# A one-core transformer kernel: constants loaded between the heads of the first batch, another split of the first projections, and a last output stage in which TensorE spreads the reciprocals

## The chip, the cores and the metric

The kernel runs on one core of one Trainium2 chip. The metric is device time in microseconds (us); the kernel before takes 2841.02 us, the median of three runs (2840.93 to 2844.28). Times in traces are counted from the start of the profiled span.

## The reference

The input x is [4, 1024, 128] in float32 (4 batches, 1024 tokens, 128 channels). Four attention blocks follow each other, each followed by a feed-forward block, each with its own layer norm and residual:

```python
x = x + attention_masked(layernorm(x))   # softmax, row i sees columns j >= i
x = x + ffn0(layernorm(x))               # x @ W[idx] + b[idx], idx = argmax(log_softmax(logits) + gumbel(u))
x = x + attention_rbf(layernorm(x))      # exp(-sigma * |k - q|^2) @ v, no softmax
x = x + ffn0(layernorm(x))
x = x + attention_rel(layernorm(x))      # Transformer-XL scores with a relative shift, softmax
x = x + ffn1(layernorm(x))               # x @ weight.T + (x[:64] + x[64:]) @ disha
x = x + attention_rope(layernorm(x))     # rotary q and k, softmax
x = x + ffn1(layernorm(x))
```

Every attention has 16 heads of 8 channels, projections q, k, v from 128 channels and an output projection back to 128.

## The kernel before

**Stages and rounds.** There are 4 stages (masked, RBF, relative, rotary) of 64 heads each (4 batches x 16), 256 heads in all. The work is laid out in rounds: round n computes the scores of head n with keys on the partitions (TensorE into `ring`, exponentials by ScalarE into `probs`), their product with the values (into `ppv`), and, two heads ahead, the scores of head n+2 with queries on the partitions, of which VectorE takes row maxima (`mx`, `mall`). Rounds -2 and -1 only take maxima. The maxima are split in three bf16 parts by GpSimd (`mparts`), turned by TensorE, copied by VectorE (`mrow`) and stored by a DMA into the query rows: that DMA is `place` (L639), and the next head's first score matmul waits for it. Sixteen rounds are an interval: while the heads of batch i-1 run, the layer norm, projections and operand splits of batch i are slipped in, and, two or more intervals later, the output projection and feed-forward of a finished batch.

**Who does what.** Layer norm: VectorE's statistics (L1284, L1287), four small GpSimd operations (L1571 to L1576), then `xn` by VectorE in the first batch and in two of the stages (L1296), otherwise by ScalarE. TensorE turns xn (L998), ScalarE copies it out (`xnT`, L1136), TensorE projects (L1013, L1020). float32 k and q are split in three bf16 parts each (cast, subtract, cast, subtract). In the first batch GpSimd splits k (L1646 to L1652) and VectorE splits q (L1356, L1358). Twelve DMAs of 256 KB store these parts to DRAM (`records_k`, `records_q`, L675), and the heads load them from there (L623, L624).

**SyncE's queue.** All DMAs are issued by SyncE, in program order: an issue behind a waiting one waits too. Constants fall in three semaphores: `s_c0` (those of the first projections and the masks), `s_ck` (for the choice of a feed-forward matrix), and `s_c1` (everything else). `s_c1` constants are issued partly before the first stores and partly right behind the first loads (L580), then 16 rows of ones (L596, L597). TensorE waits for all of `s_c1` ahead of round 0.

**The table of due times.** `Plan` gives each small step a tick (a slot of a round); every engine's program calls `start.go(tick)` and `finish.go(tick)` in each slot, which issue the steps that are due. `choose()` (L1414 to L1424) is VectorE's sum of the eight candidate matrices by a one-hot row, 19 small instructions spread over two rounds; before, it begins in round 2.

**The end.** After the last head its row of `heads_out` is stored, the denominators (`dens`) and the outputs (`oT`) of the last batch are loaded back, VectorE takes reciprocals (L1385), a DMA stores them (`inverses`), four DMAs load them spread over 8 partitions each (`den`), GpSimd multiplies (L1682), and then come output projection (L1058), residual (L1390), statistics, normalising, turning, feed-forward (L1067), residual (L1405) and the store of the result. All these matmuls go through the one PSUM bank `pm`, so that the second half of each step waits until the first has been taken out.

## Time and profile before

| what | value |
|---|---|
| median of 3 runs | 2841.02 us |
| the profiled execution, its own time | 2840.0 us |
| its span | 2838.2 us |
| PE busy | 2662.1 us (94%) |
| ACT busy | 2100.8 us (74%) |
| DVE busy | 2066.8 us (73%) |
| POOL busy | 905.8 us (32%) |
| mean granted clock of TensorE | 0.981 of full speed |

PE is TensorE, PEld its weight loads, DVE is VectorE, ACT is ScalarE, POOL is GpSimd, SPq is SyncE's DMA queue. A row of a timeline has start, duration, engine, line, operation, output and input, and in brackets the idle time of the engine before it and what ended it. The profiled execution took 1.8 us more than its span and 1.0 us less than the median of the three runs. Nearly the whole span is filled by TensorE; the stretches in which it is not are the first 71 us and the last 41 us.

### The profile page before, as it was taken

The page shows a single profiled execution, that of the slowest core. Times are in us where ns is not written, and L with a number is a line of the kernel's source. Part 1 is how long each engine was busy: PE and PEld are TensorE (multiplying, and loading weights), DVE is VectorE, ACT ScalarE, POOL GpSimd, SP SyncE. Part 2 cuts the span into 40 slices and gives each one's busy share as a digit, 9 for nine tenths or more (in the row PEclk, how much of TensorE's full clock was granted, in tenths as well). Part 3 has the DMA queues.
Part 4 walks back from the last instruction along what each step waited for, and adds up shares of the span by engine and source line. Part 5 has one row for each costly group of instructions (what it writes and reads, how often), then busy time and mean ns, then how long its engine had stood idle before and what let it go on. Part 6 is the DMA issues. An engine that isn't in the chain of part 4 may idle for free.

```text
span 2838.2 us, 107110 instructions
## 1 busy us (share of the span) xinstructions
PE 2662.1 (94%) x43744; PEld 1599.3 (56%) x43744; DVE 2066.8 (73%) x5515; ACT 2100.8 (74%) x3766; POOL 905.8 (32%) x1609
## 2 busy tenths in 40 slices
PE   3999998999999999999999999999999999999995
PEld 1666565655555555666666666666644444444443
DVE  4888888822222228888788888878889989999992
ACT  1777776799999996666666666666678878888883
POOL 2212132322213242722541361252136134351231
PEclk7999999999999999999999999999999999999997
DMA  6333232334424351411331241222123223232121
GB/s 175 88 95 116 85 109 79 112 104 127 128 88 121 96 160 55 125 57 55 97 89 50 72 131 50 72 81 70 45 64 106 63 63 98 64 112 63 57 71 40
DMA packets 197778, 250.62 MB, mean 88 GB/s; under 512 B 48340, under 2 KB 113748, under 8 KB 197288
## 3 DMA queue, kind: packets, MB, share of 16 engines
q1 hardware_dynamic: 197288, 243.77, 29.2%
q8 instruction: 346, 5.67, 0.9%
q14 instruction: 144, 1.18, 0.1%
HBM read 133.28 MB, written 100.14 MB: 82 GB/s over the span
## 4 chain that ended last, share of the span: by engine, by line
PE 69%; DVE 20%; issue 5%; ACT 2%; SPq 2%; DMA 1%; POOL 1%; DVEq 0%; ACTq 0%; POOLq 0%
PE ppv L977 29%; DVE mx L1244 14%; PE ring L834 6%; PE ring L884 6%; PE ring L819 5%; PE ring L845 4%; PE ring L917 3%; PE pm L1013 2%; DVE seen L1228 2%; DVE seen L1239 1%; PE ring L933 1%; PE pm L998 1%; PE pm L1067 1%; PE pm L1058 1%; ACT probs L1118 1%
## 5 line engine op out<-in xcount | busy, mean ns | idle before, releaser
L1118 ACT ACTIVATE probs<-ring 128x512 f32<-128x512 f32 (+1 forms) x3280 | 1969.8, 684 | 662.9 <-PE ring L834 316.0
L1244 DVE TENSOR_REDUCE mx<-ring 128x1 f32<-128x512 f32 (+2 forms) x2112 | 1284.0, 649 | 241.7 <-PE ring L884 89.4
L977 PE MATMUL ppv<-probs,values 128*32 128x128 f32 x30208 | 1146.9, 278 | 7.3 <-POOL probs L1511 2.8
L977 PEld LDWEIGHTS ppv<-probs,values 128*32 128x32 f32 x30208 | 792.8, 109 | 321.2 <-issue 163.6
L1239 DVE CUSTOM_DVE_ANT_0 seen<-ring,low_seen 128x512 f32<-128x512 f32 x576 | 392.4, 681 | 72.0 <-PE ring L884 71.6
L891 PE MATMUL ring<-kst,qst 48*128 48x512 bf16 (+1 forms) x1060 | 362.6, 391 | 37.7 <-DMA kst<-records_k 20.0
L845 PE MATMUL ring<-qst,kst 51*128 51x512 bf16 (+2 forms) x1092 | 346.2, 385 | 15.8 <-issue 11.5
L1481 POOL CAST mparts<-mall 128x8 bf16<-128x8 f32 x192 | 36.6, 191 | 826.0 <-DVE mall L1262 700.6
L884 PE MATMUL ring<-kst,qst 112*128 112x512 bf16 (+3 forms) x768 | 251.6, 328 | 11.8 <-DVE mx L1228 6.7
L1511 POOL TENSOR_SCALAR_AFFINE_SELECT probs<-probs 128x512 f32<-128x512 f32 x128 | 81.3, 635 | 564.9 <-ACT probs L1118 352.0
L834 PE MATMUL ring<-qst,kst 115*128 115x512 bf16 (+3 forms) x768 | 250.9, 327 | 0.0
L927 PE MATMUL ring<-kst,qst 48*128 48x512 bf16 x732 | 210.1, 329 | 17.8 <-DVE mx L1244 17.7
L917 PE MATMUL ring<-qst,kst 51*128 51x512 bf16 x732 | 202.8, 328 | 3.9 <-DMA qst<-mrow 3.9
L834 PE MATMUL ring<-qst_up,kst 115*128 115x512 bf16 (+3 forms) x640 | 204.0, 319 | 0.0
L884 PE MATMUL ring<-kst,qst_up 112*128 112x512 bf16 (+3 forms) x640 | 201.4, 315 | 0.7 <-DVE mx L1239 0.6
L1253 DVE COPY osb<-ppv 128x256 f32<-128x256 f32 x64 | 27.1, 424 | 202.3 <-PE ppv L977 202.3
L819 PE MATMUL ring<-qst,kst 54*128 54x512 bf16 x992 | 168.8, 384 | 0.0
L845 PEld LDWEIGHTS ring<-qst,kst 51*128 51x128 bf16 (+1 forms) x1092 | 71.4, 94 | 144.6 <-ACT probs L1118 89.0
L891 PEld LDWEIGHTS ring<-kst,qst 48*128 48x128 bf16 x1060 | 91.0, 94 | 109.1 <-DVE mx L1244 61.0
L837 PE MATMUL ring<-low_kq,identb 128*128 128x129 bf16 (+2 forms) x576 | 123.8, 215 | 0.0
L1228 DVE CUSTOM_DVE_ANT_0 seen<-ring,up_seen 128x128 f32<-128x128 f32 x512 | 117.3, 285 | 4.8 <-PE ring L876 4.1
L933 PE MATMUL ring<-hide_kq,halves 64*128 64x128 bf16 x976 | 118.9, 216 | 0.0
(165 smaller groups left out, 3002.5 us busy)
## 6 DMA issues: line engine op xcount, KB each, us to landing
qst<-records_q SPq DMA_DIRECT2D x448, 96.0 KB
heads_out<-osb SPq DMA_DIRECT2D x256, 128.0 KB, 2.0
kst<-records_k SPq DMA_DIRECT2D x320, 96.0 KB
records_k<-parts SPq DMA_DIRECT2D x96, 256.0 KB, 3.2
records_q<-parts SPq DMA_DIRECT2D x96, 256.0 KB, 3.4
kst<-records_k SPq DMA_DIRECT2D x128, 102.0 KB
oT<-heads_out SPq DMA_DIRECT2D x64, 128.0 KB, 2.7
den<-inverses SPq DMA_DIRECT2D x48, 128.0 KB, 2.6
```

Source lines behind the costliest of these rows:

```text
L819: mm = pe.matmul(bank[:, h], keys[rows, slot, kt * P:(kt + 1) * P], qs[rows, slot, h * HALF:(h + 1) * HALF], start=True, stop=True)
L834: mm = pe.matmul(bank[:, p0 - lo:p1 - lo], keys[rows, slot, kt * P:(kt + 1) * P], qq[rows, slot, p0:p1], start=p0 == lo, stop=p1 == hi and ...
L845: mm = pe.matmul(bank[:, at * P:(at + nt) * P], keys[rows, slot, kt * P:(kt + 1) * P], qs[rows, slot, q0 * P:(q0 + nt) * P], start=i == 0, ...
L884: mm = pe.matmul(bank[:, p0 - lo:p1 - lo], qq[rows, slot, qt * P:(qt + 1) * P], keys[rows, slot, p0:p1], start=p0 == lo, stop=p1 == hi)
L891: mm = pe.matmul(bank[:, at * P:(at + nt) * P], qs[rows, slot, qt * P:(qt + 1) * P], keys[rows, slot, k0 * P:(k0 + nt) * P], start=i == 0, ...
L917: mm = pe.matmul(scores[:, at * P:(at + nt) * P], keys[ROW:ROW + BASE + 3, n % SLOTS, kt * P:(kt + 1) * P], qs[ROW:ROW + BASE + 3, n % SLO ...
L927: mm = pe.matmul(tops[:, to * P:(to + mt) * P], qs_m[0:BASE, m % SLOTS, qt * P:(qt + 1) * P], keys_m[0:BASE, m % SLOTS, k0 * P:(k0 + mt) * ...
L977: mm = pe.matmul(ppv[32 * g:32 * g + 32, c:c + P], values[:, (n // H) % 2, v:v + 32], src[:, at * P:(at + 1) * P], start=u == 0 and qt < 4 ...
L1118: nc.scalar.activation(probs_of(rd.n, u), src, ACT.Exp, scale=1.0 if rd.s == RBF else SCALE).then_inc(s_exp, 1)
L1228: ins = dve.tensor_tensor_reduce(seen[:, item % 3, at * P:(at + 1) * P], bank[:, at * P:(at + 1) * P], up_seen[:, :], 1.0, 3.0 * BIG, ALU. ...
L1239: dve.tensor_tensor_reduce(seen[:, item % 3], bank[:, :], low_seen[:, first:first + HALF], 1.0, 3.0 * BIG, ALU.add, ALU.max, mx[:, slot, ( ...
L1244: ins = dve.tensor_reduce(mx[:, slot, to:to + 1], bank[:, at * P:(at + nt) * P], AX.X, ALU.max)
```

## The change

Five things change, in the program's order.

1. **Start of the first batch.** VectorE no longer waits for `s_c0` and no longer clears `work` and `values` ahead of the statistics: both memsets stand behind `xn`. GpSimd runs the four small layer-norm operations behind its first large memset (`qst`), and clears `qst_up`, `after` and `zvals` behind them. ScalarE runs a one-column copy (`warm`) at the start. The constants are put in a new order: those of the first projections ahead, the masks in a semaphore of their own (`s_cm`), for which TensorE waits only before round -2. SyncE loads one more batch of x there, no longer three.
2. **First splits.** ScalarE writes the first bf16 part of k and q straight out of PSUM (`parts[:, n, 0]`); VectorE computes the rest from PSUM (scalar_tensor_tensor: bank + bias - first part, four of 128x512), ScalarE casts the second part (two of 128x1024) and VectorE subtracts it (two of 128x1024). GpSimd has no part in it. SyncE issues the six stores of k, ScalarE's own queue the six of q.
3. **`s_c1` constants** are issued from a new generator `others()`, one every second slot from round 1 on, the 16 rows of ones at its end. TensorE waits for `s_c1` ahead of round 16, no longer ahead of round 0.
4. **`choose()`** begins in round 17, no longer in round 2.
5. **The end.** The denominators' reciprocals are not stored and loaded again: four matmuls with a 0/1 matrix (`spread`, 64 x 512, loaded in the fourth stage's first interval) spread them over the partitions, in PSUM; VectorE multiplies them with `oT` (two of 128x512). ScalarE's queue issues the loads of `oT`. The two halves of each later step have banks of their own, half the statistics run between the halves, and the result is stored in two halves.

```diff
-        SETS = 7
+        SETS = 3
...
+                        sp.dma_start(spread[:, :, :], k["spread"]).then_inc(s_tab, 16)
...
-                    for g in range(4):
-                        sp.dma_start(oT[:, g * 2 * P:(g + 1) * 2 * P], o[:, 32 * g:32 * g + D]).then_inc(s_ot, 16)
-                    if s != RBF:
+                    if j < INTERVALS:
+                        for g in range(4):
+                            sp.dma_start(oT[:, g * 2 * P:(g + 1) * 2 * P], o[:, 32 * g:32 * g + D]).then_inc(s_ot, 16)
+                    if s != RBF and j < INTERVALS:
                         yield AT["keep", j, f]
...
+            def others():
+                tick = ROUNDS[1].tick
+                def later():
+                    nonlocal tick
+                    tick += 2
+                    return tick
+                for b in range(2, B):
+                    yield later()
+                    load_x(b)
...
+                for dst, src in small:
+                    yield later()
+                    const1(dst, src)
+                yield later()
+                const_rows(RBF)
...
+                    other.go(rd.tick + u)
                     start.go(rd.tick + u)
                     finish.go(rd.tick + u)
...
+                    if j == INTERVALS:
+                        yield AT["recip", j, f]
+                        pe.wait_ge(s_rc, soft_before(f) + 1)
+                        for g in range(4):
+                            mm = pe.matmul(ring[:, 4 + g // 2, g % 2 * 2 * P:(g % 2 + 1) * 2 * P], spread[:, g], dens[:, :],
+                                           start=True, stop=True)
+                        mm.then_inc(s_bd, 1)
...
-                if rd.n == 0:
+                if rd.n == H:
                     pe.wait_ge(s_c1, NC1[0])
...
+                    if i == 0:
+                        for n in range(2):
+                            act.wait_ge(s_q0, 2 * n + 2)
+                            nc.scalar.activation(parts[:, n, 1], work[:, n], ACT.Copy).then_inc(s_a0, 1)
+                        act.wait_ge(s_q0, 6)
+                        for e in range(6):
+                            act.dma_start(records_q[0:H, e * D:(e + 1) * D], parts[:, 1, QPARTS6[e]]).then_inc(s_rec, 16)
...
+                                dve.scalar_tensor_tensor(out=work[:, n, half], in0=bank_of(name)[:, :], scalar=cols[:, col:col + 1],
+                                                         in1=parts[:, n, 0, half], op0=ALU.add, op1=ALU.subtract).then_inc(s_q0, 1)
+                        for n in range(2):
+                            dve.wait_ge(s_a0, n + 1)
+                            dve.tensor_tensor(parts[:, n, 2], work[:, n], parts[:, n, 1], ALU.subtract).then_inc(s_q0, 1)
...
+                    if j == INTERVALS:
+                        dve.wait_ge(s_bd, 1)
+                        dve.wait_ge(s_ot, 64 * (f + 1))
+                        for g in range(2):
+                            q = slice(g * HALF, (g + 1) * HALF)
+                            dve.tensor_tensor(oT[:, q], ring[:, 4 + g], oT[:, q], ALU.mult).then_inc(s_od, 1)
...
-                yield ROUNDS[2].tick
+                yield ROUNDS[H + 1].tick
                 dve.wait_ge(s_c1, NC1[0])
...
-            dve.memset(mx[:, :, :], 3.0 * BIG).then_inc(s_set, 1)
-            dve.memset(work[:, :, :], 0.0).then_inc(s_set, 1)
-            dve.memset(values[:, :, :], 1.0).then_inc(s_set, 1)
-            dve.wait_ge(s_c0, NC0[0])
+            dve.memset(mx[:, :, :], 3.0 * BIG).then_inc(s_dset, 1)
...
-            pool.memset(half_pow[:, :], -0.5).then_inc(s_set, 1)
+            pool.memset(half_pow[:, :], -0.5).then_inc(s_half, 1)
             pool.memset(qst[0][:, :, :], 0.0).then_inc(s_set, 1)
+            pool.wait_ge(s_half, 1)
+            start, finish = Steps(starts()), Steps(finishes())
+            start.go(-1)
             pool.memset(qst_up[:, :, :], 0.0).then_inc(s_set, 1)
```

GpSimd's row at the start, before (half_pow is the exponent of the layer norm's power, qst and qst_up are query buffers, shift and rstd belong to the layer norm):

```order
L1694 MEMSET half_pow 128x8
L1695 MEMSET qst 128x4096
L1696 MEMSET qst_up 128x4096
L1697 MEMSET after 128x288
L1698 MEMSET zvals 128x192
L1571 TENSOR_SCALAR shift<-meanvar 128x8
L1572 TENSOR_SCALAR rstd<-meanvar 128x8
L1574 TENSOR_TENSOR rstd<-rstd,half_pow 128x8
L1576 TENSOR_TENSOR shift<-shift,rstd 128x8
L1646 CAST parts<-proj 128x1024
L1648 TENSOR_TENSOR work<-proj,parts 128x1024
```

and now:

```order
L1769 MEMSET half_pow 128x8
L1770 MEMSET qst 128x4096
L1650 TENSOR_SCALAR shift<-meanvar 128x8
L1651 TENSOR_SCALAR rstd<-meanvar 128x8
L1653 TENSOR_TENSOR rstd<-rstd,half_pow 128x8
L1655 TENSOR_TENSOR shift<-shift,rstd 128x8
L1774 MEMSET qst_up 128x4096
L1775 MEMSET after 128x288
L1776 MEMSET zvals 128x192
L1560 CAST mparts<-mall 128x8
```

The three memsets moved from ahead of the layer norm's operations to right behind them, and the split of k (L1646 and on) is gone.

SyncE's queue from the loads of round 8 to those of round 9 (records are stores of the next batch's parts), before:

```order
L623 DMA qst<-records_q 48x1024
L624 DMA kst<-records_k 48x1024
L675 DMA records_q<-parts 16x8x1024 x2
L644 DMA heads_out<-osb 128x256
L639 DMA qst<-mrow 3x8x128
L675 DMA records_q<-parts 16x8x1024 x3
```

and now:

```order
L638 DMA qst<-records_q 48x1024
L639 DMA kst<-records_k 48x1024
L692 DMA records_q<-parts 16x8x1024
L595 DMA cols<-in_L_attn_b_bk 128x1
L692 DMA records_q<-parts 16x8x1024
L659 DMA heads_out<-osb 128x256
L595 DMA bv<-in_L_attn_b_bv 128x128
L654 DMA qst<-mrow 3x8x128
L692 DMA records_q<-parts 16x8x1024
L595 DMA zmask<-in_zmask 128x8
L692 DMA records_q<-parts 16x8x1024
L595 DMA heads_of<-in_heads_of 128x16
```

Two constants now stand ahead of the round's `place` (qst<-mrow), and two or three behind it.

## Rows read from the trace of the kernel before

**Rows 1.** Timeline of the first 75 us, all engines.
```profile
4.28 3.51 POOL L1696 MEMSET qst_up<- 128x4096 bf16 x1
...
9.71 0.49 DVE L1284 BATCH_NORM_STATS2 stats<-x 128x6 f32<-128x128 f32 x2 [4.06 <-DMA hide_kq<-in_hide_kq]
...
14.68 2.14 DVE L1296 TENSOR_SCALAR xn<-x,meanvar,rstd 128x128 f32<-128x128 f32 x8 [2.72 <-POOL shift L1576]
...
19.06 3.78 PE L1013 MATMUL ring<-xnT,wk 128*128 128x512 f32 x4 [1.06 <-ACT xnT L1136]
...
25.54 0.69 ACT L1164 ACTIVATE proj<-ring,cols 128x512 f32<-128x512 f32 x1 [0.27 <-PE ring L1013]
...
31.41 3.86 SPq L675 DMA_DIRECT2D records_k<-parts  x6
...
31.97 1.23 DVE L1358 TENSOR_TENSOR parts<-work,parts 128x1024 bf16<-128x1024 f32 x1
...
43.20 0.33 SPq L623 DMA_DIRECT2D qst<-records_q  x1
...
56.49 0.20 DVE L1272 COPY mrow<-ring 24x128 bf16<-24x128 bf16 x1
...
71.11 0.58 PE L845 MATMUL ring<-qst,kst 51*128 51x512 bf16 x1 [11.53 <-issue]
```

**Rows 2.** Chain of waits, first 220 us: start, us, what.
```profile
17.12 1.28 ACT L1136
...
60.68 6.77 DMA tables<-in_tables
```

**Rows 3.** Timeline of the last 41 us, all engines.
```profile
2802.64 1.75 DVE L1385 RECIPROCAL dens<-dens 64x256 f32<-64x256 f32 x1 [15.98 <-DMA dens<-heads_out]
...
2813.30 2.05 PE L1058 MATMUL pm<-wo,oT 128*128 128x128 f32 x8 [15.88 <-POOL oT L1682]
2815.45 0.69 DVE L1390 TENSOR_TENSOR x<-pm,x 128x512 f32<-128x512 f32 x1 [11.07 <-PE pm L1058]
...
2821.06 0.30 DVE L1287 BATCH_NORM_AGGREGATE meanvar<-stats 128x2 f32<-128x6 f32 x2
...
2828.15 0.60 ACT L1136 ACTIVATE xnT<-pm 128x512 f32<-128x512 f32 x1 [1.21 <-PE pm L998]
...
2834.55 0.41 SPq L713 DMA_DIRECT2D out_x<-x  x1
```

**Rows 4.** DMA issues of 0.5 to 1.3 us: KB each, us to landing.
```profile
x<-in_L_attn_a_x SPq DMA_DIRECT2D x1, 512.0 KB, 4.2
```

**Rows 5.** DMA view of 31 to 43.5 us, the stretch of the first stores.
```profile
DMA packets 1728, 3.15 MB, mean 252 GB/s; under 512 B 192, under 2 KB 192, under 8 KB 1728
```

**Rows 6.** Timelines of POOL and of DVE, 1100 to 1110 us.
```profile
1103.08 0.64 POOL L1511 TENSOR_SCALAR_AFFINE_SELECT probs<-probs 128x512 f32<-128x512 f32 x1 [2.04 <-PE ring L884]
...
1103.12 0.68 DVE L1296 TENSOR_SCALAR xn<-x,meanvar,rstd 128x128 f32<-128x128 f32 x1
```

**Rows 7.** Chain of waits, 340 to 500 us: a late place, issue to landing.
```profile
453.60 2.02 DMA qst<-mrow
```

**Rows 8.** Timeline of SyncE's queue, round 9: its first load and its place.
```profile
144.26 0.59 SPq L623 DMA_DIRECT2D qst<-records_q  x1
...
148.59 0.77 SPq L639 DMA_DIRECT2D qst<-mrow  x1
```

**Rows 9.** Timeline of SyncE's queue, a round with a gather: its first load.
```profile
445.55 0.32 SPq L623 DMA_DIRECT2D qst<-records_q  x1
```

**Rows 10.** Who waited for whom, 430 to 460 us: total, times, longest.
```profile
PE ring L917 <- DMA qst<-mrow: 1.7, 1, 1.7
```

**Rows 11.** Windows: us, busy (x) of PE, PEld, DVE, ACT, POOL, PEclk, DMA, GB/s.
```profile
200.00:207.00 7.00, 6.72 (x125) 4.41 (x123) 6.62 (x20) 4.83 (x10) 3.02 (x8) 1.00 0.27 78
...
86.70:95.80 9.10, 8.15 (x142) 5.45 (x143) 8.78 (x26) 8.74 (x20) 0.90 (x4) 1.00 0.21 61
...
151.00:158.00 7.00, 6.70 (x134) 4.57 (x134) 6.15 (x14) 5.17 (x11) 0.78 (x4) 1.00 0.25 78
```

More of the change, by code:

```diff
@@ L370, in pool_ops_to @@
 def pool_ops_to(i):
-    return sum(POOL_OPS[k // B] if k else 4 for k in range(i))
+    return sum(POOL_OPS[k // B] for k in range(1, i))
 class Steps:
@@ L427, in build @@
         tables = sb("tables", [P, 4, T])
+        spread = tables[0:4 * H, 3, 0:4 * P].rearrange("p (g q) -> p g q", g=4)
         squares = tables[:, 2].rearrange("p (t c) -> p t c", t=NT)
@@ L433, in build @@
         half_pow = sb("half_pow", [P, NT])
+        warm = sb("warm", [P, 1])
         mx = sb("mx", [P, SLOTS, 4 * NT])
@@ L510, in build @@
         s_db = sem("s_db")
+        s_bd = sem("s_bd")
+        s_od = sem("s_od")
         s_at = sem("s_at")
@@ L709, in finishes @@
                                          .to_broadcast([H, D, 2 * P])).then_inc(s_db, 16)
-                    if s == STAGES - 1:
+                    if j == INTERVALS:
+                        for h in range(2):
+                            sp.wait_ge(s_pc, FILL["fill", j, f, "ff", h] + 1)
+                            sp.dma_start(out[b].rearrange("(t p) c -> p t c", p=P)[:, 4 * h:4 * h + 4], x[:, b, 4 * h:4 * h + 4]).then_inc(s_fin, 16)
+                    elif s == STAGES - 1:
                         yield AT["done", j, f]
@@ L1185, in finishes @@
                     yield from turned_norm(j, f, "tf")
+            act.wait_ge(s_half, 1)
+            nc.scalar.activation(warm[:, :], half_pow[:, 0:1], ACT.Copy)
             act.wait_ge(s_c0, NC0[0])
@@ L1272, in copy_max, with statistics @@
                 dve.tensor_copy(mrow[:, :], ring[:, rd.turned() % 3].bitcast(BF16)[0:3 * NT, 0:P]).then_inc(s_sm, 1)
-            def statistics(name, w, count, b):
+            def statistics(name, w, count, b, first=0, end=NT + 1):
                 done = sum(not centred_by_pool(interval_of(f)) for f in range(count)) if w == "f" else count
-                for t in range(NT + 1):
+                for t in range(first, end):
                     yield AT[*name, t]
@@ L1699, in _ @@
             pool.wait_ge(s_set, SETS)
-            start, finish = Steps(starts()), Steps(finishes())
-            start.go(-1)
+            pool.wait_ge(s_dset, 3)
             for rd in ROUNDS.values():
@@ L1774, in shape_constants @@
         "up_seen": hide(i[None, :] < i[:, None] + 2),
+        "spread": np.where(np.arange(4 * H)[:, None, None] == H * np.arange(4)[None, :, None] + i[None, None, :] // D, f(1), f(0)).astype(f),
         "zmask": np.where((i[:, None] == P - 1) & (np.arange(NT)[None, :] == NT - 1), f(BIG), f(0)).astype(f),
```

194 lines of the change are left out of this document (108 added, 86 removed).

## The prediction, made before the changed kernel was run

> **What bounds the kernel now.** I read the page first: TensorE is busy 94% of the span, so a change is worth something only where TensorE stands still. The timeline of the first 75 us and the chain of waits show the one such place, the last 41 us the other; the rounds between are full. At the start the reader is to see a string of hand-overs. VectorE begins its statistics at 9.71 us, after 4.06 us of idleness that a mask constant ended, though it needs only x [rows 1]. xn begins at 14.68, the projections at 19.06, the first store is issued at 31.41, and the first load, which waits for all stores, at 43.20 [rows 1]. TensorE takes maxima from there and then idles 11.53 us until 71.11 [rows 1]; the chain runs through the last big constant, the tables, in that gap [rows 2]. At the end the reciprocal ends at 2804.39, the output projection starts at 2813.30 only, and the rest is a ladder of halves that wait for each other in one bank [rows 3].
>
> **The change part by part.** The sum is made against the profiled execution's own time, 2840.0 us; the median of the runs is 1.0 us above it.
>
> *A, up to the first load (43.20).* Step 1, the constant. x is issued at 0.79 (the first issue of all) and lands 4.2 us later [rows 4], at about 5.0; with VectorE's long memsets moved away and GpSimd's first memset over by then, the statistics start there: 9.71 - 5.0 = 4.7 us gained. Step 2, the table load. ScalarE's 1.28 us load stands on the chain at 17.12 [rows 2] and goes with the warm-up copy; as TensorE is still turning the second half until about 18.0, the projections (19.06) gain only 1.0. Step 3, the splits. The last projection is taken out at 26.23 [rows 1]; on that axis, less the 1.0, at 25.2. The VectorE operations out of PSUM for k and the first half of q lie between the projections and cost nothing: what hides them is TensorE, which gives a bank only every 1.9 us (3.78 for two [rows 1]). Then in a row: ScalarE's cast of 128x1024, not in this trace; bounds are 0.7 (one 128x512 out of PSUM, 0.69 [rows 1]) and 1.4 (two), I take 1.05; VectorE's subtraction, 1.23 as at 31.97 [rows 1]. The stores of k start at 27.6 in place of 31.41, so steps 2 and 3 give 3.8. The stores of q follow 1.25 later, on the other queue. Step 4, the stores. Before, 3.15 MB [rows 5] took 11.8 us from the first issue to the first load. The six issues of k cost 3.86 [rows 1]; two queues issue at once now. By issue alone it would be 1.25 + 3.9 + about 3.5 for a landing, 8.7; by the transfers: the mean of 252 GB/s over 12.5 us [rows 5] has some 2.5 idle us at its ends, so 10 us of flow; with two issuers filling the queues I take 9, and 1.4 around them, 10.4. The larger decides: 1.4 gained.
> The rule of the Trainium skill on this (DMA: Bandwidth & Descriptors, Issuing engines are not separate DMA queues) is that a second issuing engine saves only issue time, as all go to the same 16 engines. By it step 4 gives 1.4; were the queues separate paths, about 3. The sum goes by the row.
>
> Step 5 is a new wait. The memset of qst_up, 3.51 us [rows 1], now stands right behind the GpSimd operation that releases xn. In the trace eight xn take 2.14 [rows 1], 0.27 each, but one that began at 1103.12, 0.04 after a GpSimd operation of 0.64 us on a large tile, took 0.68 and ended at 1103.80, just behind that operation's end at 1103.72 [rows 6]. So xn does not run beside such an operation, it waits for it. GpSimd's memset needs no semaphore trip and starts some 0.08 us ahead of xn: xn waits 3.4 us. Bounds: 0 (a memset reads nothing, and no row here has xn beside one) and 4.4 (also the two small memsets behind it, 0.34 and 0.26, and slower xn). I take 3.5; xn, turning, projections and everything behind it shift by it.
> The Trainium skill states the mechanism (SBUF — State Buffer, Who interferes with whom): a VectorE operation in a two-port mode and a GpSimd operation exclude each other for a whole instruction, and whichever is issued first wins. By that rule, the two rows agree; without it step 5 would be 0.
>
> A in all: 4.7 + 3.8 + 1.4 - 3.5 = 6.4 gained (ends 5 and 11).
>
> *B, ahead of round 0.* The gap of 11.53 [rows 1] ends with constants. They are gone from there; what is late next is place of round -1: mrow is ready at 56.7 [rows 1], its issue is not held up any more, it lands 2.02 later [rows 7], 58.8, while TensorE works to 59.6. So the whole gap goes: 11.5 (ends 10 and 12). For TensorE's clock, which could be granted sooner without the gap, I count nothing; a faster round 0 would be a gain of 1 to 2 us on top, inside the range.
>
> *C, the constants in rounds 1 to 11.* 42 more issues and, in round 10, 16 rows of ones enter SyncE's queue. An issue of a load took 0.33 at one place and 0.59 at another [rows 1, 8]; I take 0.47 for a constant and the shorter for a row of ones. The trace has no such rounds; it has the limit. In round 9 place is issued 4.3 us after the first load [rows 8] and lands in time. In a round with gathers it came 8.05 after (445.55 to 453.60 [rows 7, 9]) and TensorE idled 1.7 [rows 10]. So up to about 6.3 is free, and each us beyond costs one. A constant or two ahead of place alone (0.9) are hidden by this slack. But in rounds 6 to 9 the queue also issues stores of 0.64 each (3.86 / 6 [rows 1]): a round with five of them holds SyncE for 6.6 of 7.0 us, four or five constants make it 8.8 to 9, and the surplus is carried on. Followed through the new order, place is 2.0 late in round 7, 1.7 in round 8, 2.9 in round 9; beyond the 1.5 to 1.8 that are free this is 0.5 + 0.2 + 1.4 = 2.1 lost. Bounds 0 (constants squeeze into idle time) and 6 (2 us more in the fullest rounds, as the wait of 1.7 on a jam [rows 10] can come twice, and once more). I take 2.1, the value of the nearest rows.
>
> *D, choose().* Its first 13 instructions leave round 2, where VectorE is busy 8.78 of 9.10 us with 26 instructions, and go to round 17, where it is busy 6.62 of 7.00 [rows 11]. A plain round has 14 instructions and 6.15 us [rows 11], so the 13 cost 2.6; 6.62 + 2.6 = 9.2, no cover is left, and the round becomes 2.2 longer. Round 2 gains 0.1, since ScalarE (8.74) holds it as long. The other 6 go into a round of 9 us with 7.5 busy and are hidden. D costs 2.1 (ends 0 and 3).
>
> *E, the end.* The reciprocal ends at 2804.39. Four matmuls of 256 columns follow: 1024 columns took 3.78 at the start [rows 1], 512 took 2.05 at this place [rows 3]; I take 3.6 (2.1 if the clock were full, 4.1 by the second row). Two multiplications out of PSUM, 0.69 each [rows 3], 1.5 with the hand-over. Output projection starts at 2809.5, 3.8 earlier than 2813.30. The halves then follow each other without waiting: 4.1 for both, the second addition and the remaining statistics 2.1; before, from 2813.30 to 2821.36, 8.1 [rows 3], so 1.9 gained. Turning: 0.7; the second feed-forward half no longer waits for the first addition: 0.8. The store of half the result saves 0.3 behind the last addition. Five steps: 3.8 + 1.9 + 0.7 + 0.8 + 0.3 = 7.5; 0.2 off for loads of oT that now run beside those of the denominators. E gives 7.3 (ends 5 and 9.5).
>
> Sum: -6.4 - 11.5 + 2.1 + 2.1 - 7.3 = -21.0. Own time 2819.0, median 2820.0.
>
> **The rivals.** R1, the memset does not hold xn up. For it: no row has that pair. Against it: the xn of 0.68 [rows 6]. Then step 5 is 0: 2816.5. R2, SyncE's queue falls further behind: the 512 KB tables of rounds 9 and 10 go out right ahead of place, and the 16 rows of ones (16 x 0.33, 5.3 us) delay round 11's loads by over 3. For it: an earlier queue jam did cost TensorE 1.7 [rows 10]. Against it: two such rounds cost little in all. With the upper bound of C and 2 more for late loads, C is 8: 2826. R3, the end gives less: the loads of oT on the second queue delay the denominators by a microsecond or two, and the spreading takes its upper bound; E is 4: 2823.3. R4, slower than before: each constant holds the queue not 0.47 but 2 us; then a round has 9 us of constants beside 3 of its own against 7.0, 5 too many in each of 9 rounds, 45 lost where C has 2.1: 2863. Rounds 1 to 10 leave SyncE about 42 us idle, one for each constant, so it decides from about 1.5 us an issue on (42 x 0.5 is the whole gain of 21). Against it: the two issues above are at most 0.59, and the six stores took 0.64 each [rows 1]. R5, the change doesn't do what it says: B is not gained, because another wait (loads of round 0, ScalarE's small chain for the choice) ends as late; 2831. Against it: that chain ends 3 us before it is needed.
>
> **How the numbers follow.** Forecast 0.48, R1 0.25, R2 0.11, R3 0.10, R5 0.03, R4 0.03. The range takes in R1, the forecast with its own spread of 3 us either side, R3 and most of R2: 2812 to 2828. A measurement of this kernel tells about 0.2% (5.7 us) from no change. Every case but R4 is faster by more than that: faster 0.96; same 0.01; slower 0.03.
>
> **What the profile of the changed kernel would show.** Statistics at 5.0. xn's first instruction 3.5 us long, or started 3.5 after GpSimd's last small operation (R1: 0.3 long). The first load at about 36.8 (R1: 33.3). No gap of TensorE ahead of round 0, which starts about 17.9 earlier than 71.11, at 53.2. TensorE waiting for qst<-mrow in rounds 7 to 9, some 2 us. A round 17 of 9.2 us, busy on VectorE. From the reciprocal's end to the output projection 5.1 us (before 8.9), and to the issue of the last store 23.2 (before 30.2). I am wrong if the first load comes before 34 or after 39, if waits for mrow sum to over 5 us, or if the time from the last head to the end shrinks by under 5.

## The result, and the profile after

| | kernel before | changed kernel |
|---|---|---|
| median, first comparison | 2843.05 us (7 runs) | 2827.63 us (7 runs, 2820.36 to 2839.28) |
| median, second comparison | 2841.42 us (7 runs) | 2829.46 us (4 runs) |
| profiled execution, own time (span) | 2840.0 (2838.2) | 2820.36 (2818.6); second trace 2833.71 (2832.0) |
| mean granted clock of TensorE in it | 0.981 | 0.986; second trace 0.981 |

The ratio is 0.9942 with a 95% interval of 0.9919 to 0.9966, and 0.9954 (0.9937 to 0.9970) in the second comparison. So the change makes the kernel 0.5% faster. The forecast was 2820.0, range 2812 to 2828. The direction is right; the median of the first comparison lies just inside the range, that of the second just outside it. That the first trace took 2820.36 is, as shown below, two errors that cancelled.

**The start.** Timeline of the changed kernel's start, all engines (the rows that answer to [rows 1]):

```profile
5.33 0.49 DVE L1351 BATCH_NORM_STATS2 stats<-x 128x6 f32<-128x128 f32 x2 [4.28 <-DMA x<-in_L_attn_a_x]
...
10.21 3.51 POOL L1774 MEMSET qst_up<- 128x4096 bf16 x1
10.31 5.37 DVE L1363 TENSOR_SCALAR xn<-x,meanvar,rstd 128x128 f32<-128x128 f32 x8 [2.72 <-POOL shift L1655]
...
24.95 5.79 SPq L692 DMA_DIRECT2D records_k<-parts  x6
...
26.09 7.47 ACTq L1222 DMA_DIRECT2D records_q<-parts  x6
...
36.74 0.34 SPq L638 DMA_DIRECT2D qst<-records_q  x1
...
52.82 0.60 PE L878 MATMUL ring<-qst,kst 51*128 51x512 bf16 x1
```

Statistics wait for x and begin at 5.33 (before 9.71). xn begins 0.10 us after GpSimd's memset and takes 5.37 us for eight, against 2.14 [rows 1]. The first load comes at 36.74 (before 43.20), and the row of round 0 shows no idle time before it: TensorE begins it at 52.82 (before 71.11).

**Rounds 6 to 11.** Chain of waits of the changed kernel, 104 to 160 us; start, duration, what. A row of `DMA qst<-mrow` runs from the issue of a `place` to the matmul that waited for it:

```profile
110.66 2.58 DMA qst<-mrow
...
119.77 2.91 DMA qst<-mrow
...
136.59 2.65 DMA qst<-mrow
...
142.80 6.22 DMA qst<-mrow
```

The trace of before has no such row here (its one late place is [rows 7]). TensorE's waits in this stretch:

```profile
PE ring L950 <- DMA qst<-mrow: 6.2, 4, 2.7
```

The numbers are us in total, times, and the longest. A place can be late in two ways: it stands in the queue after its data is ready, or it is long on its way. The data is ready at the end of VectorE's copy `mrow`; for round 7 its row is

```profile
116.51 0.20 DVE L1339 COPY mrow<-ring 24x128 bf16<-24x128 bf16 x1
```

so that the place issued at 119.77 had stood in the queue for 3.06 us. Those of rounds 6 and 9 stood for 1.27 and 1.89 us. That of round 10, at 142.80, stood for 0.09 only and was long on its way. The four waits are 0.23, 2.36, 0.92 and 2.70 us.

And behind two of the four waits the granted clock falls to its lower level. Windows of the changed kernel, around the place issued at 119.77 and around that of 142.80 (columns as in [rows 11]):

```profile
119.80:122.20 2.40, 0.57 (x10) 0.30 (x5) 0.77 (x3) 0.19 (x1) 0.79 (x4) 1.00 0.60 174
122.20:125.60 3.40, 2.87 (x32) 1.91 (x33) 1.89 (x3) 1.68 (x3) 0.00 (x0) 0.53 0.45 124
...
145.50:149.00 3.50, 0.86 (x19) 0.59 (x10) 1.06 (x4) 0.48 (x1) 0.79 (x4) 1.00 0.85 304
...
150.00:153.30 3.30, 3.30 (x41) 2.14 (x40) 1.74 (x4) 1.73 (x5) 0.00 (x0) 0.53 0.36 105
```

TensorE was busy 0.57 of 2.40 us and 0.86 of 3.50 us, and then worked for 3.4 us at about 1.2 instead of 2.4 GHz. If TensorE could have used the full clock all that time, each of the two falls costs 1.7 us (an estimate). With the waits that makes 6.2 + 3.4 = 9.6 us, and this stretch lost 9.4, as the table below shows. In the second trace it is 7.1 us of waits and 10.2 us at the lower clock, 12.2 by the same sum, and 11.4 lost.

**The end.** Timeline of the changed kernel's last 34 us (answering to [rows 3]):

```profile
2784.89 0.38 ACT L1155 ACTIVATE osb<-ppv 128x256 f32<-128x256 f32 x1 [0.55 <-PE ppv L1010]
...
2787.65 2.03 SPq L714 DMA_DIRECT2D dens<-heads_out  x4
2787.69 2.56 ACTq L1246 DMA_DIRECT2D oT<-heads_out  x4
2791.82 1.74 DVE L1457 RECIPROCAL dens<-dens 64x256 f32<-64x256 f32 x1 [17.75 <-DMA dens<-heads_out]
...
2793.62 3.78 PE L1089 MATMUL ring<-dens,tables 64*128 64x256 f32 x8 [8.80 <-DVE dens L1457]
2797.43 1.29 DVE L1463 TENSOR_TENSOR oT<-ring,oT 128x512 f32<-128x512 f32 x2 [3.87 <-PE ring L1089]
...
2798.87 3.45 PE L1104 MATMUL ring<-wo,oT 128*128 128x128 f32 x16 [1.47 <-DVE oT L1463]
...
2814.18 2.11 SPq L731 DMA_DIRECT2D out_x<-x  x2
```

From the reciprocal's end (2793.56) to the output projection it is 5.3 us (before 8.9, forecast 5.1), to the last store's issue 22.3 (before 30.2, forecast 23.2). But the reciprocal itself starts 6.9 us after the last copy `osb`, where before it was 5.2.

**The ledger.** SyncE's first load of each round is a clock that both kernels have. Reading off how much earlier each one comes than before gives the terms by stage (us, minus is gained; the first trace adds up to its -19.6 us, the second to -6.2):

| term, and where it is read | forecast | first trace | second trace |
|---|---|---|---|
| A, to the first load | -6.4 | -6.5 | -6.6 |
| B, to the first load of round 6 | -11.5 | -11.7 | -10.3 |
| C, rounds 6 to 11 | +2.1 | +9.4 | +11.4 |
| D, round 17 | +2.1 | +1.5 | +1.5 |
| round 18 to the last head | 0 | -5.2 | +4.6 |
| E, behind the last head's load | -7.3 | -7.1 | -6.8 |

A, B, D and E are right within 1.2 us, A and E by errors that cancel, as the step-by-step part says. C is 7 to 9 us too small. Six more traces of kernels that leave rounds 6 to 11 alone lose 7.0 to 10.2 us there, so that C scatters by 4.4 us over eight traces. And the rounds that the change does not touch differ by 10 us between two executions of the same kernel.

### The profile page after: what moved, and what is told of

The parts are those of the page before. It is cut to its first block, busy times and chain, and to the rows that moved or that the text cites. A ratio compares the mean times of both kernels' runs of the same rounds, so it can differ in the third digit from the quotient of the medians.

```text
span 2818.6 us, 107129 instructions
## 1 busy us (share of the span) xinstructions
PE 2662.6 (94%) x43752; PEld 1600.2 (57%) x43752; DVE 2070.0 (73%) x5519; ACT 2103.6 (75%) x3769; POOL 898.3 (32%) x1604
## 4 chain that ended last, share of the span: by engine, by line
PE 69%; DVE 20%; issue 5%; ACT 2%; DMA 1%; SPq 1%; POOL 0%; ACTq 0%; DVEq 0%; POOLq 0%
PE ppv L1010 29%; DVE mx L1311 14%; PE ring L867 6%; PE ring L917 6%; PE ring L852 5%; PE ring L878 4%; PE ring L950 3%; PE pm L1050 2%; DVE seen L1295 2%; DVE seen L1306 1%; ACT probs L1167 1%; PE ring L966 1%; PE pm L1035 1%; PE pm L1113 1%; PE pm L1104 1%
## 5 line engine op out<-in xcount | busy, mean ns | idle before, releaser
L917 PE MATMUL ring<-kst,qst 112*128 112x512 bf16 (+3 forms) x768 | 251.5, 328 | 11.8 <-DVE mx L1295 6.7
```

The lines of the kernel that those rows point to most:

```text
L917: mm = pe.matmul(bank[:, p0 - lo:p1 - lo], qq[rows, slot, qt * P:(qt + 1) * P], keys[rows, slot, p0:p1], start=p0 == lo, stop=p1 == hi)
```

## The experiments

Each starts from the changed kernel and is named by its one edit. Where only one execution was timed, its trace's ledger is the evidence, not its time.

**Again, unchanged.** Is the 5.2 us in the untouched rounds the change's doing?

> The changed kernel, unchanged, a second time. Up to SyncE's first load of head pair 42 (the 43rd of the run, after choose()) the trace should repeat the first within 0.5 us at each head: first load 36.7, round 0 at 52.8, 9.5 us lost in rounds 6 to 11. The 5.4 us by which the first trace gained on the kernel before between round 20 and the last head are chance by one theory (single late heads of 1 to 3 us, which fall elsewhere in each execution): then the last head ends 2 to 8 us later than 2784.9 here, and the profiled time is 2822 to 2829. By the rival (the change itself makes the later rounds faster) the last head ends within 1.5 us of 2784.9.

Measured: 2829.46 us median. The profiled execution took 2833.71, above the 2822 to 2829 that I gave, and its last head came 13.0 us later than in the first trace where I gave 2 to 8. So those 5.2 us were chance. Head by head the second trace falls back in single steps, and at most of them the granted clock is down. First two of TensorE's rows and the window behind them at one such place of the second trace, then the same of the first:

```profile
485.27 0.39 PE L960 MATMUL ring<-kst,qst 48*128 48x512 bf16 x1 [1.84 <-DVE mx L1311]
...
486.46 1.46 PE L1057 MATMUL pm<-wv,xnT 128*128 128x128 f32 x8 [0.69 <-DVE values L1435]
...
487.00:490.40 3.40, 3.40 (x40) 2.61 (x39) 2.02 (x6) 0.60 (x1) 0.34 (x2) 0.53 0.13 37
```

```profile
481.15 0.39 PE L960 MATMUL ring<-kst,qst 48*128 48x512 bf16 x1 [1.84 <-DVE mx L1311]
...
482.35 1.16 PE L1057 MATMUL pm<-wv,xnT 128*128 128x128 f32 x8 [0.69 <-DVE values L1435]
...
484.00:487.40 3.40, 3.40 (x50) 2.57 (x51) 2.81 (x6) 1.72 (x4) 1.94 (x6) 1.00 0.40 116
```

TensorE waits the same 1.84 and 0.69 us at the same two instructions in both; one execution drops to half clock (the lower level) behind them and the other does not, and loses 1.6 us against it between the first loads of rounds 52 and 54. Summed over the stretch that no edit here touches, from the first load of head 32 to that of the last head, the time at the lower clock and the length of the stretch go together in all 14 traces of this case:

| us at the lower clock | traces | length of the stretch, us |
|---|---|---|
| 13.7 | the first of the changed kernel | 2456.1 |
| 20.5 | three | 2458.5 to 2459.7 |
| 23.9 | that of before, and the best version's | 2461.4 and 2461.7 |
| 27.3, 30.7 | two, one | 2462.4 to 2464.8 |
| 34.1 | four, the second of the changed kernel among them | 2464.2 to 2466.0 |
| 64.9 | one | 2477.4 |

A straight line through them (2451.1 us and 0.42 for each us at the lower clock) misses none by more than 1.2 us. That the two go together doesn't show which causes which; the pair of traces above shows that the same waits can be followed by either clock. In the last row of the table most is one long stretch, whose window is

```profile
1050.00:1084.00 34.00, 34.00 (x220) 11.19 (x220) 17.30 (x53) 12.43 (x21) 1.08 (x6) 0.50 0.08 25
```

That is the scatter of this kernel, and the time of one execution tells nothing below 10 us.

**Constants early, rows of ones spread.**

```diff
-                    tick += 2
+                    tick += 1
...
-                yield later()
-                const_rows(RBF)
...
+                for n in range(2 * SLOTS):
+                    yield ROUNDS[H - 4 + n // 4].tick + 2 * (n % 4)
+                    rbf_row(n // 2, ROW * (n % 2))
```

> Constants one every slot from round 1 on (over by round 6, when the stores begin) in place of one every second slot, and the 16 rows of ones two at a time in rounds 12 to 15. Theory (SyncE's queue is too full in rounds 6 to 10, where stores and constants meet): the waits of TensorE for qst<-mrow in rounds 6 to 11 go from 9.5 us to under 1, the head times of round 12 come 9 us earlier, median 2818 to 2820. Rival 1 (42 more issues cost the queue their time wherever they stand): the loss moves to rounds 1 to 5 and stays at 5 to 10 us. Rival 2 (the transfers of the constants, not the issues, make the place land late): the wait moves with them too, and issue to landing of the place is over 3 us.

Measured: 2818.42 us median (4 runs), ratio to the kernel before 0.9918 (0.9903 to 0.9933). Rounds 6 to 11 lose 1.2 us; the two places behind the tables, now in rounds 5 and 6, are what is left:

```profile
103.30 3.74 DMA qst<-mrow
111.38 2.87 DMA qst<-mrow
```

The loss did not move to rounds 1 to 5, so rival 1 falls: the same 42 issues cost nothing where the queue carries no stores. These five rounds take 44.4 us here, and 44.2 to 44.4 in four traces of kernels that leave them alone and whose lower clock at the start lasts 37.5 us, as it does here; the first trace, with 34.1 us of it, has 43.3. Rival 2 holds for the place of round 5, right behind tables, where it gave over 3 us. As the edit moves constants, tables and rows of ones together, it doesn't part the issues from the transfers of stores and constants.

**Only the rows of ones spread.**

> Constants as in the changed kernel; only the 16 rows of ones are taken from their one slot and go two at a time in rounds 12 to 15. Theory (the burst holds the queue for 5.2 us and delays the loads and the place of the next round): the 2.9 us lost between the first loads of rounds 10 and 12 go, those of rounds 6 to 9 (6.6 us) stay. Rival (these 2.9 us are the backlog of rounds 6 to 9, handed on): under 1 us is gained at round 12.

Measured: the burst was not it. Rounds 6 to 11 lose 11.6 us, as much as in the second trace. With SyncE free behind round 10, the place issued at 144.90 still let TensorE wait to 152.09. First its row in the chain of waits, then TensorE's timeline:

```profile
144.90 7.14 DMA qst<-mrow
```

```profile
152.09 0.61 PE L958 MATMUL ring<-qst,kst 51*128 51x512 bf16 x1 [3.66 <-DMA qst<-mrow]
```

So this place was late on its way, not in the queue of issues. Its edit is the lower half of the diff above.

**Only the tables moved.**

```diff
-                small += [(tables[:, n], k["tables"][n]) for n in range(4)]
...
+                for n in range(4):
+                    yield ROUNDS[H - 4 + n].tick + ROUNDS[H - 4 + n].turn + 1
+                    sp.dma_start(tables[:, n], k["tables"][n]).then_inc(s_ct, 16)
...
```

GpSimd waits for `s_ct` before the tables' first reader. The edit moves something else too: with four constants fewer, the burst of 16 rows of ones comes eight slots earlier.

> The changed kernel with one edit: the four tables (512 KB each) leave their slots in rounds 9 and 10 and go one a round in rounds 12 to 15, right behind place. In the changed kernel the place issued at 142.80, behind the tables, let TensorE start only at 149.06; in the kernel in which the rows of ones were taken away (and the tables stayed) this wait was still there, 3.7 us. Theory (the 2 MB of transfers ahead of it in the queue delay that place): TensorE's wait of 2.7 us near 149 and the half clock behind it go, 3 to 4 us less are lost between the first loads of rounds 9 and 12; the 6.2 of rounds 6 to 9 stay. Rival (the issues ahead of place and the backlog of rounds 6 to 9 delay it): under 1 us is gained, or the wait comes back in rounds 12 to 15.

Measured: the theory holds, with less gained than it said. The place of round 10 is issued later and arrives in a third of the time:

```profile
145.27 1.99 DMA qst<-mrow
```

It is issued later because the burst now stands ahead of it, from 137.13 to 142.16: the place stood in the queue for 3.4 us, and TensorE still waited 1.75 us for it, against 2.70. So the burst, which costs nothing behind the place, costs something ahead of it. Rounds 6 to 11 lose 6.6 us (three waits of 4.9 us in all and one fall of the clock, 1.7), and rounds 12 to 15, with a table each right behind place, lose nothing. One trace of a stretch that scatters from 7.0 to 11.6 us would prove little by its sum; the way of the place proves more. From its issue to the matmul that waits, it took 4.9 to 7.1 us in all nine traces in which the tables stand ahead of it in rounds 9 and 10, and 1.99 us here. From the first load of round 9 to that of round 12 those nine lose 2.0 to 5.9 us, this one 0.8.

So C has two parts. Some 2 to 3 us come by 2 MB of tables ahead of a 6 KB transfer. The changed kernel's DMA view of 137 to 150 us lists the tables so (KB each, us to landing),

```profile
tables<-in_tables SPq DMA_DIRECT2D x4, 512.0 KB, 5.8
```

and some 5 to 6 in the rounds where stores and constants meet. Both count the half clock that follows a wait. Alternating with stores a constant took 0.58 or 0.59 us, a store and a constant together 1.20 to 1.26 from start to start, and single issues 1.46 and 1.63. Timeline of SyncE's queue in the changed kernel, rounds 6 and 8:

```profile
105.69 1.46 SPq L638 DMA_DIRECT2D qst<-records_q  x1
...
112.08 1.63 SPq L595 DMA_DIRECT2D wv<-in_L_attn_a_Wv  x1
...
130.25 0.59 SPq L595 DMA_DIRECT2D heads_of<-in_heads_of  x1
130.88 1.46 SPq L692 DMA_DIRECT2D records_q<-parts  x1
```

**GpSimd's memsets behind xn.**

```diff
             start.go(-1)
+            pool.wait_ge(ln["a"]["xn"], NT)
             pool.memset(qst_up[:, :, :], 0.0).then_inc(s_set, 1)
```

> GpSimd waits for all eight xn before it clears qst_up, after and zvals. Theory (the memset holds VectorE's xn for its whole length): the eight xn take 2.1 us in place of 5.4, TensorE turns from 11.6 in place of 14.8, the first load comes at 33.5 in place of 36.7, and the time is 3.2 us less. Rival 1 (VectorE's first xn is long for another reason, such as a first use of its operands): xn still takes 5.4. Rival 2 (what is behind it is late anyway: GpSimd's memsets now end at 16.4): the first load comes at 35 or later.

Timeline of its start:

```profile
9.85 2.14 DVE L1363 TENSOR_SCALAR xn<-x,meanvar,rstd 128x128 f32<-128x128 f32 x8 [2.71 <-POOL shift L1655]
...
33.22 0.34 SPq L638 DMA_DIRECT2D qst<-records_q  x1
```

GpSimd's memset begins behind it, at 12.05. xn takes 2.14 us again, 3.23 less, and the first load comes at 33.22, 3.52 us earlier than in the first trace. Step 5 of the forecast (3.5) is confirmed; the tenth is luck, as the first load of the ten traces that keep the memset there ranges from 35.82 to 36.87.

**The memset in eight pieces.**

```diff
-            pool.memset(qst_up[:, :, :], 0.0).then_inc(s_set, 1)
+            for slot in range(SLOTS):
+                for h in range(2):
+                    ins = pool.memset(qst_up[:, slot, h * HALF:(h + 1) * HALF], 0.0)
+            ins.then_inc(s_set, 1)
```

> The memset of qst_up is cut into eight of 128x512 (0.44 us each), at the same place. By the theory of a lock that one instruction holds from its start to its end, xn gets its turns between the pieces: the first xn starts or ends under 1 us after GpSimd's last small operation, single xn are 0.3 to 0.8 us long, and the fourth is done 1 to 2 us earlier than now. By the rival of a shared bandwidth, all eight xn are stretched alike while the memsets run; by a second rival, that GpSimd wins every turn, the first xn is still 3.5 us long.

I had expected xn to get its turns; it got none. Timeline, and the view of the tile xn (durations in ns, min/median/max):

```profile
9.96 3.79 POOL L1776 MEMSET qst_up<- 128x512 bf16 x8
10.05 5.85 DVE L1363 TENSOR_SCALAR xn<-x,meanvar,rstd 128x128 f32<-128x128 f32 x8 [2.72 <-POOL shift L1655]
```

```profile
L1363 DVE TENSOR_SCALAR xn<-x,meanvar,rstd x8: 328/335/4249, 10.1 to 15.6; 128x128 f32<-128x128 f32 x8
```

The first xn is 4.25 us long, over eight memsets and the small ones behind them, and the other seven are short. The second rival holds: back-to-back GpSimd instructions keep VectorE out as one long one does. The Trainium skill (SBUF — State Buffer, Who interferes with whom) says that whoever issues first holds the shared ports for the whole instruction; the trace agrees for one instruction (3.8 us in the changed kernel), and goes further for a row of them.

**Stores of q by SyncE again.**

```diff
-                            if i or g == 0:
-                                sp.dma_start(dst[lo:lo + H, e * D:(e + 1) * D], parts[:, part, which[e]]).then_inc(s_rec, 16)
+                            if True:
+                                sp.dma_start(dst[lo:lo + H, e * D:(e + 1) * D], parts[:, part, which[e]]).then_inc(s_rec, 16)
...
-                        for e in range(6):
-                            act.dma_start(records_q[0:H, e * D:(e + 1) * D], parts[:, 1, QPARTS6[e]]).then_inc(s_rec, 16)
```

> The six stores of q go behind the six of k on SyncE's queue again, in place of ScalarE's. In the changed kernel each of the twelve issues took 0.97 and 1.25 us on two queues, against 0.64 on one, and the stretch from the first store to the first load is 11.8 us as before. Theory (the transfers, 3.15 MB, set this stretch, not the issues): it stays within 0.6 us of 11.8, first load at 36.2 to 37.3. Rival (my prediction's step 4: a second queue saves 1.4): 13.2 us, first load at 38.1.

Timeline, SyncE's queue:

```profile
24.50 3.88 SPq L692 DMA_DIRECT2D records_k<-parts  x6
28.42 4.93 SPq L692 DMA_DIRECT2D records_q<-parts  x6
36.30 0.34 SPq L638 DMA_DIRECT2D qst<-records_q  x1
```

From the first store to the first load it is 11.80 us, against 11.79 with two queues and 11.79 before: the second queue gives nothing. Two queues at once each issue more slowly: in the changed kernel six issues took 5.79 us on SyncE and 7.47 on ScalarE, here 3.88 and 4.93. So the forecast's 1.4 falls. That the transfers set the 11.8 us is the likely reason; it is argued, not shown.

**oT by SyncE at the end.** The changed kernel's loads of oT go back behind those of the denominators (the condition `if j < INTERVALS` and ScalarE's four issues taken out).

> At the end SyncE issues the four loads of oT behind those of the denominators, ScalarE none. Theory (the loads of oT on a second queue, 0.5 MB at the same time, delay the denominators): from the end of the last copy of outputs to the start of the reciprocal 5.2 us in place of 6.6 (5.16 less 0.38 before, 6.93 less 0.38 in the changed kernel), oT lands before the spreading ends, and the end is 1.7 us shorter. Rival 1 (the denominators' landing is late by chance): no change. Rival 2 (oT now lands behind the spreading, 7 us after its first issue): the multiplication starts later, and nothing is gained.

Timeline of its end:

```profile
2795.09 0.38 ACT L1155 ACTIVATE osb<-ppv 128x256 f32<-128x256 f32 x1 [0.55 <-PE ppv L1010]
...
2799.62 2.52 SPq L717 DMA_DIRECT2D oT<-heads_out  x4
2800.95 1.75 DVE L1449 RECIPROCAL dens<-dens 64x256 f32<-64x256 f32 x1 [16.68 <-DMA dens<-heads_out]
```

The reciprocal starts 5.9 us after the start of that copy (6.9 and 7.3 in the changed kernel's two traces, 5.2 before), and the end behind the copy is 32.4 us instead of 33.7 and 34.1. oT is there in time. One trace alone gives 1.3 of the expected 1.7 us. In the two kernels below that have this edit too, the reciprocal starts 5.2 and 5.3 us after the copy, in the ten traces with oT on ScalarE's queue 6.5 to 7.3. So it is 1.6 us in the mean: R3's mechanism is real.

**choose() thin, rounds 17 to 25.**

```diff
-                    yield ROUNDS[H + 1].tick + 2 * e
+                    yield ROUNDS[H + 2 + e].tick + 2
```

> choose() spreads its 19 small instructions over rounds 17 to 25, at most three in a round, in place of 13 in one. Theory (a round has 0.85 us in which VectorE idles; only more than that costs): round 17 takes 7.0 to 7.5 us as its neighbours, and the 1.45 us lost there go. Rival (VectorE's idle time in a round is made of waits that the work behind inherits): the same 1.5 us are lost, in several rounds.

Measured: 11 us lost in rounds 21 to 25, which neither theory had. Timeline of GpSimd and VectorE in round 21:

```profile
234.06 2.13 POOL L1690 TENSOR_TENSOR parts<-work,parts 128x1024 bf16<-128x1024 f32 x1
234.39 1.94 DVE L1507 SCALAR_TENSOR_TENSOR wf<-oT,pick,wf 128x128 f32<-128x128 f32 x1
```

A 128x128 instruction of 0.35 us takes 1.94 and ends 0.14 behind the end of GpSimd's subtraction. It looks like the same hold as that of the memset: these rounds are those in which GpSimd splits k and q. Rounds 21, 22 and 23 have one such instruction each (1.94, 1.78 and 1.86 us), take 3.1 to 3.8 us longer than in the first trace, and the granted clock falls to its lower level for 3.4 us in each. That the maxima queue up behind it and TensorE waits for them is the likely path; the next run tests the cause.

**choose() in rounds 12 to 16**, where GpSimd does little.

> choose() alone moved: five of its instructions in round 12, four each in rounds 13 to 15, two in round 16. The spreading over rounds 17 to 25 lost 11 us in rounds 19 to 25, where single 128x128 instructions took 1.8 to 1.9 us beside an operation of GpSimd. Theory (that was GpSimd's hold on VectorE; rounds 12 to 16 have only GpSimd's four small operations of 0.2 us each): each instruction takes 0.2 to 0.35, rounds 12 to 16 lose 0 to 0.6 in all, round 17 is 7.45 us as before the change, 1.5 gained. Rival (any instruction more on VectorE delays the maxima): 1 to 3 us lost in rounds 12 to 16.

Measured: each instruction takes 0.28 to 0.37 us now, as the theory says, but rounds 12 to 16 lose 2.5 us, as the rival says. The 0.85 us that VectorE idles in a plain round is no cover. That its idle time lies in front of maxima that TensorE waits for would explain it; no run takes this apart. (The trace is the one with 34 us at half clock, at 1050 us, far from the edit; its 2842.32 us says nothing of it.)

**All mends, and the best version.** The first had choose() in rounds 12 to 16:

> All mends together: constants one every slot from round 1; the four 512 KB tables out of s_c1, one a round in rounds 12 to 15 right behind place, the rows of ones behind them; GpSimd's memsets behind xn; choose() at most five instructions a round in rounds 12 to 16, where GpSimd has no long operation; oT loaded by SyncE behind the denominators. Against the changed kernel: 3.5 from the memsets, 7.3 to 9 from rounds 6 to 11, 1.5 to 3 from choose(), 1.3 from the end, 13.6 to 17 in all: median 2811 to 2815, first load at 33.2, under 1 us lost between the first loads of rounds 1 and 17. By the rival (each late place only moves to another round, and TensorE's granted clock drops somewhere else instead) 2816 to 2822.

Measured: 2814.44 us median (2808.66 to 2817.93), ratio 0.9900 (0.9883 to 0.9916). Rounds 2 to 11 lose nothing; rounds 12 to 16 lose 4.1 us with choose(), of which round 17 gives 0.4 back. I had said under 1 us between rounds 1 and 17. The denser constants are not quite free either: a place issued at 64.05, right behind two loads of x of 512 KB each, was late. TensorE's row:

```profile
68.42 0.39 PE L962 MATMUL ring<-qst,kst 51*128 51x512 bf16 x1 [1.27 <-DMA qst<-mrow]
```

The second has choose() in rounds 18 and 19:

> As the kernel with all mends, but choose() whole in rounds 18 and 19 (13 and 6 instructions), the rounds of batch 2's start that answer to rounds 2 and 3, where the kernel before had it. Spread over rounds 12 to 16 it lost 3.6 to 4.1 us of head time (2.5 where it was the only edit); bunched in round 17 it lost 1.45. Round 2 with it took 9.1 us in the kernel before and 8.9 us without it in the changed kernel, as ScalarE, busy 8.6 us, holds that round. Theory (a round that ScalarE bounds hides it): rounds 12 to 19 lose 0.2 in all, median 2810 to 2812, about 3 less than the kernel with all mends. Rival (VectorE's work is never hidden here, each added instruction costs 0.13 us): 2.5 us lost in rounds 18 and 19, median 2813 to 2815.

Measured: **2809.94 us** median (4 runs, 2808.27 to 2812.0) against 2839.99 before; ratio 0.9889 (0.9872 to 0.9905). Rounds 17 to 20 lose 0.2 us, no TensorE instruction between 60 and 165 us waits for a place, and the first load stands at 33.4. It beats both kernels: 30 us less than the kernel before, and 15 to 18 us less than the changed one by the ratios.

## Why the prediction was right or wrong, step by step

**Step 1** (4.7): 4.4; statistics wait for x, which lands 0.3 us later. Right. **Steps 2 and 3** (3.8): 5.6. That is what is left of A with the other steps as measured. The splits cost what was said (cast 1.0, subtraction 1.2), but the last projection is taken out at 22.7 instead of 26.2, 3.5 us earlier, where steps 1, 2 and 5 had 2.2. Most of the difference is TensorE's clock, of which the forecast had nothing here. Single projections of k and q (duration in ns, min/median/max), before and then in the changed kernel:

```profile
L1013 PE MATMUL ring<-xnT,wk x4: 1061/1061/1222, 19.1 to 21.8; 128*128 128x512 f32 x4
L1013 PE MATMUL ring<-xnT,wq x4: 593/896/1061, 22.6 to 24.9; 128*128 128x512 f32 x4
...
L1050 PE MATMUL ring<-xnT,wk x4: 914/1061/1221, 16.6 to 19.4; 128*128 128x512 f32 x4
L1050 PE MATMUL ring<-xnT,wq x4: 592/592/593, 20.1 to 21.4; 128*128 128x512 f32 x4
```

In each kernel their length falls from 1061 to 592 ns at one moment: at 24.6 us before, in the middle of q's four, and at 20.0 us now, ahead of all of them. The trace's list of granted clocks begins at just these moments, with the full clock, so a window that shows 1.00 ahead of them shows only that nothing is recorded there. q's four projections take 1.88 us in place of 2.87 by it. TensorE's first matmul stands at 15.94 us before and at 14.80 now.

**Step 4** (1.4): nothing, shown by the stores experiment; the larger of two bounds was the right choice, but the bound itself should have been the measured 11.8 us, which I had split into flow and ends on no evidence. **Step 5** (-3.5): confirmed by taking it away. A came out at 6.5 since 1.8 too little and 1.4 and 0.3 too much cancel: that is luck. Rival R1 falls.

**B** (11.5): right in the first trace and in three more with 34.1 us of lower clock at the start (11.7 to 11.9); 10.1 to 10.4 with 37.5 us of it, 9.1 and 9.6 with 41.0. (With all mends it was 10.2 at 34.1 us of it, with the wait of 1.27 us.) R5 falls.

**C** (2.1, bounds 0 and 6) is the step that failed: 9.4 and 11.4, and 7.0 at the least. How long place stands in the queue was about right in sum: 2.0, 1.7 and 2.9 us in rounds 7 to 9 were forecast, and 1.3, 3.1, 0.0 and 1.9 in rounds 6 to 9 were measured. Three other things were wrong. First, I took 1.5 to 1.8 us of lateness as free; it was 0.7 to 1.0 (3.06 late cost 2.36, 1.89 cost 0.92, 1.27 cost 0.23), since place took 2.6 to 2.9 us on its way in place of 2.02. So rounds 6 to 9 have waits of 3.5 us, not 2.1. Second, the transfer was priced at 2.02 us however much lay ahead of it in the queue; behind the tables it was 6.22, a wait of 2.7. Third, I counted each us of waiting once, where TensorE's clock fell to half behind two of the four waits, for up to 1.7 us each. R2, with a chance of 0.11, came nearest. It named the tables right ahead of place and the burst of ones and priced C at 8; the tables were real, the burst was not where the change has it. I had written that waits for mrow over 5 us in sum would show me wrong: they were 6.2.

**D** (2.1): 1.5; right in kind. The round took 7.45 us before, not the 7.00 that the forecast's window showed, and became 8.90 where I said 9.2. In five other traces of these kernels the clock falls to half for 3.4 us there, and it costs 3.0.

**E** (-7.3): -7.1, right in sum by two errors. The spreading took 3.78 us (3.6). From the reciprocal's end to the end of the span 8.7 us were gained where five steps gave 7.5; the reciprocal itself starts 1.8 us later behind the last copy, where I took 0.2 off.

**The sum.** -21.0 was forecast; without the untouched rounds the traces give -14.3 and -10.8, and the medians say -15.4 and -12.0. The forecast's own spread of 3 us left out that the rounds untouched by the change scatter by 5 us either way, which one trace cannot show. That the first median still fell in the range is luck in part: its upper end had been drawn for R2, and the second median, 2829.46, lies beyond it. R4 falls: most constants took 0.42 to 0.60 us to issue, and only single ones 0.9 to 1.6.

## What to carry to other kernels

Count a queue shared by small urgent and large patient transfers twice: by its issues, and by the bytes ahead of the urgent one; put the large ones right behind it. A wait of TensorE is paid again in part where its clock falls behind it, so count the falls with the waits. And before a VectorE instruction is moved, look at what GpSimd runs there.

## What the runs showed of the hardware that I had not expected

- Eight back-to-back GpSimd memsets of 0.47 us kept a VectorE tensor_scalar out for all of them (4.25 us).
- The same work, with the same waits, falls to half clock in one execution and not in another. Outside the edited rounds, 13.7 to 64.9 us at half clock go with a stretch 0.42 us longer for each, and that line leaves 1.2 us at most of 21 us of scatter.
- Two queues issuing large stores at once are no faster than one: 11.8 us for 3.15 MB either way. The Trainium skill (DMA: Bandwidth & Descriptors, Issuing engines are not separate DMA queues) says that a second issuing engine saves only issue time; here not even that was saved, since each issue took longer.
- A projection of 128x512 takes 1061 ns up to one moment and 592 ns behind it, 24.6 us into the kernel before and 20.0 us into the changed one. Where the profile has no record yet, its granted clock reads 1.00 all the same; the durations of single matmuls tell the level.
